# ScalarE copies the high part of an attention group's output before, not after, it stores a row of maxima

## The reference

```python
x = _attn(_ln(x, g1, b1), _ln(x, g1, b1), Wq1, Wk1, Wv1, Wo1, bo1) + x
# in _attn: 16 heads of 64, scale = 64 ** -0.5
scores = jnp.einsum('bnhd,bshd->bhns', q, k) * scale
attn = jax.nn.softmax(scores, axis=-1)
out = jnp.einsum('bhns,bshd->bnhd', attn, v).reshape(B, N, HEADS * D_HEAD)
```

## Time and profile before

| | |
|---|---|
| median of 3 runs | 3405.64 us |
| lowest and highest run | 3403.01 and 3417.11 us |
| the profiled execution | 3418.57 us, of which the span is 3416.8 us |
| granted TensorE clock over the span, mean | 0.959 |
| busy: TensorE matmuls / VectorE / ScalarE / GpSimd | 93% / 67% / 53% / 32% of the span |
| first self attention | about 185 to 572 us of the span |

### The profile page before, as it was taken

The page is one execution under the profiler, slowest core; times in us unless marked ns, Lnnn a source line. Parts: engine busy times, 40 slices in busy tenths (PEclk is TensorE's granted clock), DMA queues, the critical chain, the costliest instruction groups (busy, mean ns, idle before and its releaser), DMA issues. The chain is left out here.

```text
span 3416.8 us, 48174 instructions
## 1 busy us (share of the span) xinstructions
PE 3163.9 (93%) x17084; PEld 1853.1 (54%) x17084; DVE 2278.1 (67%) x4098; ACT 1805.3 (53%) x3369; POOL 1087.7 (32%) x537
## 2 busy tenths in 40 slices
PE   7968886999969999999999989979999699999989
PEld 5834443788844555555555567733568444444357
DVE  5447775434447777777777655579766599999844
ACT  4424444444424444444444534447756278888864
POOL 1036664000036787777787800002200000000000
PEclk9979998999969999999999999979999689999999
DMA  6897874999896666667666432254635622323140
GB/s 229 311 207 211 216 211 169 364 337 343 294 230 144 151 149 150 152 158 163 150 150 150 140 137 99 87 168 133 226 127 198 223 89 89 113 84 111 59 144 26
DMA packets 367127, 588.80 MB, mean 172 GB/s; under 512 B 47152, under 2 KB 197216, under 8 KB 365736
## 3 DMA queue, kind: packets, MB, share of 16 engines
q1 hardware_dynamic: 361844, 582.43, 57.7%
q10 hardware_dynamic: 5044, 3.29, 0.4%
HBM read 344.19 MB, written 241.29 MB: 171 GB/s over the span
## 5 line engine op out<-in xcount | busy, mean ns | idle before, releaser
L2265 ACT ACTIVATE a_prob<-a_ring 128x512 f32<-128x512 f32 (+1 forms) x1088 | 552.3, 618 | 466.5 <-PE a_ring L2171 462.7
L2299 DVE TENSOR_REDUCE a_blk_max<-a_ring 128x1 f32<-128x402 f32 x1024 | 517.7, 569 | 281.8 <-PE a_ring L2155 281.1
L1790 ACT ACTIVATE a_prob<-a_ring 128x512 f32<-128x512 f32 (+1 forms) x1088 | 582.2, 605 | 136.8 <-PE a_ring L1712 130.8
L2112 POOL TENSOR_TENSOR a_prob_sum<-a_prob,a_prob_sum 128x1024 f32<-128x1024 f32 x256 | 602.1, 2396 | 2.1 <-ACT a_prob L2265 2.1
L1835 DVE TENSOR_REDUCE a_blk_max<-a_ring 128x1 f32<-128x402 f32 x1024 | 506.9, 567 | 34.7 <-PE a_ring L1699 27.9
L2184 PE MATMUL a_pv<-a_prob,a_v 128*64 128x512 f32 (+1 forms) x2176 | 505.2, 603 | 0.0
L2170 PE MATMUL a_ring<-a_q_stack,a_k_stack 128*128 128x512 f32 (+1 forms) x1088 | 456.8, 420 | 19.2 <-DMA a_q_second<-maxima 13.2
L2171 PE MATMUL a_ring<-a_q_second,a_k_second 65*128 65x512 f32 (+1 forms) x1088 | 438.5, 403 | 0.0
L2112 POOL TENSOR_TENSOR a_prob_sum<-a_prob 128x1024 f32<-128x1024 f32 x128 | 301.8, 2368 | 397.4 <-DVE a_chunk_sum L2331 199.8
L1730 PE MATMUL a_pv<-a_prob,a_v 128*32 128x256 f32 (+2 forms) x4096 | 341.1, 406 | 13.7 <-ACT a_prob L1790 7.8
L1699 PE MATMUL a_ring<-a_k_stack,a_q_stack 63*128 63x402 f32 (+1 forms) x1280 | 281.7, 423 | 38.6 <-DMA a_q_stack<-q_lo_self 17.6
(11 more groups left out here) (270 smaller groups left out, 4811.7 us busy)
## 6 DMA issues: line engine op xcount, KB each, us to landing
a_k_stack<-k_hi_cross SPq DMA_DIRECT2D x96, 400.5 KB, 4.5
a_v<-v_cross SPq DMA_DIRECT2D x48, 768.0 KB
a_k_stack<-k_lo_cross SPq DMA_DIRECT2D x80, 400.5 KB, 6.0
a_k_second<-k_hi_cross SPq DMA_DIRECT2D x32, 801.0 KB, 12.4
v_cross<-p_v_sb SPq DMA_DIRECT2D x48, 512.0 KB
k_hi_cross<-p_split_hi SPq DMA_DIRECT2D x120, 200.0 KB, 3.5
k_lo_cross<-p_split_lo SPq DMA_DIRECT2D x120, 200.0 KB, 4.2
a_q_stack<-q_hi_self SPq DMA_DIRECT2D x64, 256.0 KB, 4.5
```

Source lines behind the costliest of these rows:

```text
L1790: nc.scalar.activation(prob[0:keys, tau % RC, m, :], ring[0:keys, score_place(e) % BANKS, :], ACT.Exp, scale=a.scale).then_inc(exp_done, 1)
L2112: nc.gpsimd.tensor_tensor(prob_sum[:, h], prob_of(i * NCP + cp, h), other, ALU.add)\
L2265: nc.scalar.activation(prob_of(w, h)[0:keys, ch % 2, :], ring[0:keys, score_bank(e), :], ACT.Exp, scale=a.scale).then_inc(exp_done, 1)
L2299: nc.vector.reduce_max(dst, ring[:, max_bank(g), 0:a.blk], AX.X).then_inc(item_read, 1)
```

## The change

In ScalarE's program the block with the two `high_part` calls is put in front of the block with `load_maxima` and `store_maxima`. In the self attention this alters the turns with `cp == 1`: for groups 2 to 29 the order "store the row of maxima of group i + 2, copy the high part of group i - 2" becomes "copy, store". Groups 30 and 31 have no store. `load_maxima` stands at `cp == 0`, where no copy is, and keeps its place. In the cross attention both blocks never meet, so its program is the same.

```diff
                         nc.scalar.activation(prob_of(w, h)[0:keys, ch % 2, :], ring[0:keys, score_bank(e), :],
                                              ACT.Exp, scale=a.scale).then_inc(exp_done, 1)
+                if cp == 4 and i:
+                    high_part(i - 1)
+                elif cp == NCP - 1 and not a.cross and i >= 2:
+                    high_part(i - 2)
                 if not a.cross and cp == 0 and 1 <= i < NG - 1:
                     load_maxima(i + 1)
                 elif not a.cross and cp == 1 and i < NG - 2:
                     store_maxima(i + 2)
-                if cp == 4 and i:
-                    high_part(i - 1)
-                elif cp == NCP - 1 and not a.cross and i >= 2:
-                    high_part(i - 2)
             if not a.cross:
                 raw_copy(NG - 2)
                 high_part(NG - 2)
```

## The result

The changed kernel took 3380.09 us (median of 4 runs, 3368.72 to 3384.79) against 3411.38 us for the kernel before (4 runs, 3403.01 to 3426.01): a ratio of 0.9899, 95% interval 0.9854 to 0.9944. Timed again beside two variants, six runs, it gave 0.9893 (0.9871 to 0.9915). The profiled execution took 3378.85 us, with a span of 3377.0 us where the one before had 3416.8.

The account below looks back on a forecast made before the run. TensorE, the fullest engine, was taken to stand still 1.2 us a turn behind ScalarE's late copy. 27 turns x 1.20 = 32.4 us off 3405.64 gave 3373.2 us, range 3364 to 3395.

Parts of the forecast that it names:

- The mechanism: ScalarE's copy to o_hi waits 3.2 us behind the store of the maxima, delaying the low part and TensorE's denominators.
- the count: The stall exists in 27 turns of the first self attention, from 3 to 29.
- the term per turn: Each steady turn of the first self attention gains 1.20 us, 32.4 us over 27 turns.
- the high end of a turn's gain: TensorE's whole stall in a turn, 1.23 us, or 33.3 us from the total of the waits.
- The copy moved ahead costs nothing: On ScalarE the copy runs from about 391.65 to 392.24 us, inside old idle time, covered by 2 us.
- The store moved behind costs nothing: On ScalarE the store still waits for VectorE's turn at 394.18 and is issued at 394.22 us: 0 us.
- The low part: On VectorE it follows the turn by 0.06 us, from 394.24 to 394.93 us instead of from 395.44.
- TensorE's loop, 9.99 us: One turn on TensorE: 5.34 us from blocks' matmuls to values, 3.65 for values, 1.00 for denominators.
- VectorE's loop ends last, by a hair: VectorE's chain through the low part and denominators to the next blocks takes 10.02 us and sets the turn.
- Rival 1, the loads: DMA loads set the turn: at the fill's 223 GB/s it takes 10.77 us, kernel 3379 to 3393 us; chance 0.13.
- Rival 2, the row of maxima: Row lands late, holding four exponentials: near 3400 us, chance 0.09, or near 3421 us, chance 0.04.
- Rival 3: The copy still waits because the quotient comes only in the turn's later half: no change, 3405.6 us; chance 0.02.

Follow-up runs that it names:

- e8: Changed kernel with ScalarE's copy of the high part moved further ahead, in front of the second four exponentials: 3486.3 us, turn 13.666 us.
- e1: Changed kernel with VectorE's low part after two of the four blocks instead of behind all four: 3373.26 us, in five rounds 3375.20 us, turn 9.777 us.
- e6: Changed kernel plus one useless 128x512 addition on VectorE ahead of each low part: 3404.37 us, turn 11.149 us.
- e4: Changed kernel plus a second store of o_hi by SyncE to a scratch tensor, 256 KB more each turn: 3378.44 us, turn 9.850 us.
- e3: Changed kernel with the store of the maxima right before the load of the same row, behind four exponentials: 3546.38 us, turn 16.2 us on average.
- e2: Changed kernel with the store of the maxima put behind the raw copy of the next turn: 3375.01 us, turn 9.850 us.
- e7: Kernel before with ScalarE's copy left in place and the store of the maxima issued by SyncE instead: 3378.66 us, turn 9.854 us.
- e9: e1 with TensorE multiplying the first chunk's values before the first four blocks of maxima: 3381.68 us, ratio 0.9900, turn 9.936 us.

## Why the prediction was right, and where its sizes were off

The mechanism, its place and the count held. 3373.2 us was forecast, 0.95% less than the median of before; 3380.09 and a ratio of 0.9899, 1.01% less, came, inside the range. How near the number comes is partly luck: the medians differ by 31.3 us, beside 32.4 forecast, while the turns of the trace gained 36.3; and the median of before, 3405.64 us then, is 3411.38 with one run more. In the trace the turn was to go from 11.23 to 10.02 or 10.03 us and went to 9.85, so the term per turn, 1.20 us, measured 1.39, and 32.4 us in the turns measured 36.3. That is also more than the 1.23 us that the prediction took for the high end of a turn's gain: the wait in the earlier trace rows is counted from the modelled end of the values, while from start to start the step shrank by 1.37 us. That the medians differ by less than the turns gained lies within the scatter of the rest of the program, which in these executions varies by several microseconds; the repeat's ratio of 0.9893 is 36.5 us.

Step by step:

- *The copy moved ahead costs nothing.* Right: it starts as the exponentials end, and its idle time names nothing more. e8 shows that its cover is just this place.
- *The store moved behind costs nothing.* Right: issued at 395.40, just behind the transpose of 395.15.
- *The low part.* Mis-sized. I let it start 0.06 us after the transpose's end, by the gap between the blocks and the transpose. It starts 0.07 us before that end. The transpose reads what the blocks wrote, the low part reads nothing of the transpose, and where that was so the earlier trace rows already had an overlap (multiplication until 391.56, blocks from 391.46). It took 0.65, not 0.69: together 0.17 us.
- *TensorE's loop, 9.99 us.* Mis-sized: I put 3.65 us for the values, the time to the last modelled end. What counts in a chain is the distance of the starts, 3.51 us in the changed kernel, 3.49 in e1. The denominators, 1.00 in the sum, take 0.96 where they wait for nothing. TensorE's loop is 9.78 us.
- *VectorE's loop ends last, by a hair.* Right in rank, as e6 (all of 1.28 us passed on) and e1 (0.075 us gained) show. In the trace of the changed kernel alone it can't be seen, since TensorE appears busy without a gap.
- *Rival 1, the loads.* Wrong in its premise. The 223 GB/s of the fill were no ceiling: 243 were held after the change and 270 in e4. I had taken the rate of a stretch with hardly any stores for the capacity of a mix with stores. Slices 8 to 10 of the page of the kernel before, which lie in a later stage with other transfers, already had 337 to 364 GB/s. The gap in the DMA engines' work did vanish, as forecast, and nobody waited for it.
- *Rival 2, the row of maxima.* The mechanism is real (e3), and its length was no false fear: 6.52 us in the fill, up to 6.2 in e3. In the changed kernel it struck once, in the fill: a load 6.28 us after its store and 2.95 after its first exponential, and values that started 10.81 us after those of the turn before. It shows as the first distance of 10.80 us. In the steady turns the load kept its 1.33 us, and by e2, with the DMA engines at the same share of 0.92, 3.60 us would have been enough. Why the row is quick there is not shown; the queues were not empty, since from each store to its load the DMA engines' share was 0.81 to 1.08 (250 to 490 us). The rule of the Trainium skill ("DMA: Bandwidth & Descriptors", "Issuing engines are not separate DMA queues"), that transfers of both queues run on the same engines and interleave, fits the 5.12 to 6.19 us of e3, and it cost nothing where the change puts the store.
- *Rival 3.* Excluded by e7 and by the trace.

## What to carry to other kernels

An instruction that waits in an engine's queue delays everything behind it, however unrelated. When a wait names a releaser whose data the waiting instruction does not read, look at what stands ahead of it in the queue; then order each queue by the time at which the inputs come, not by the order in which the steps were thought of (e7, and e8 for the other side).

Where a chain of starts is added up, take distances between starts, not busy times. And before a busy resource is called the next limit, load it a little more: the extra store showed in one run that DMA engines at a share of 0.92 were no limit, and the extra addition that a VectorE with idle time was one.

## What the runs showed of the hardware that was not expected

- A wait of TensorE has a second price. Waits of 1.49 us (e8) and 1.62 us (e3) were followed by a granted clock of 0.50 and values that took 5.21 and 5.35 us instead of 3.65. In the kernel before, the wait of 1.23 us in each turn left the clock at 1.00. The length of the wait alone does not decide it: in the fill of e2 a wait of 1.18 us was followed by 0.50 and values of 5.05 us.
- The DMA engines moved 270 GB/s at a share of 1.02, while in the fill they moved 223 GB/s at 1.03. The share does not tell the rate.
- An addition of 128x512 elements on VectorE with both inputs in SBUF took 1.33 to 2.00 us in the 30 cases in which GpSimd was at work beside it, 1.34 in most, and 0.69 us in the two last ones, where GpSimd stood still (e6). Instructions of the same size with one input in PSUM took 0.65 to 0.70 us. The Trainium skill, page "SBUF — State Buffer", section "Who interferes with whom", says that VectorE instructions with two SBUF inputs contend with GpSimd's reads; the trace of e6 agrees, and in the three longest cases of 1.68, 1.99 and 2.00 us GpSimd's next addition took 1.60 instead of 1.27 us too.
- Between the last score's matmul and the next kind of matmul 0.32 to 0.33 us pass, whether that next one depends on exponentials of the group or not (e1, e9), where most steps between scores take 0.23 to 0.24. It is not the change of kind alone: the step from the first score's matmul to the second takes 0.34 us (397.53 to 397.87 in e1).
